# Scores from three bf16 parts on 96 rows, the causal zeros from GpSimd, and one maximum for a pair of heads

## What is computed

```python
q = (layernorm(x) @ w_q.T)  -> 16 heads of 16      # x: (16, 256, 256)
k, v = ctx @ w_k.T, ctx @ w_v.T
scores = einsum('bhqd,bhkd->bhqk', q, k) / sqrt(16)
weights = softmax(where(tril, scores, -inf))
x = x + (weights @ v) @ w_o.T
...
x = x + softmax(q2 @ k2.T / 16) @ v2               # q2, k2, v2: routed two-layer networks of layernorm(x)
```

## Time and profile before

| | us |
|---|---|
| median of three runs | 658.51 |
| lowest and highest | 652.58, 661.08 |
| span of the profiled execution, first to last instruction | 656.6 |
| own time of the profiled execution | not told apart from the three runs; the span is 1.9 below their median |
| ramp, up to the first scores of step 0 | 0 to 38.6 |
| steps 0 to 14 of the pipeline | 39.5 to 377.7 |
| step 15, the tail and the tables | 377.7 to 435 |
| routed networks | 435 to about 540 |
| second attention | about 540 to 656.6 |

### The profile page before, as it was taken

One profiled execution on the slowest core, in us unless ns is written; L12 is line 12 of the kernel. 1 busy time (PEld: TensorE's weight loads), 2 busy tenths in 40 slices (PEclk: granted clock), 3 DMA queues, 4 the chain that ended last, 5 costly groups with the idle time before them and its releaser, 6 DMA issues.

```text
span 656.6 us, 14722 instructions
## 1 busy us (share of the span) xinstructions
PE 587.3 (89%) x5119; PEld 500.4 (76%) x5119; DVE 450.4 (69%) x1511; ACT 294.5 (45%) x482; POOL 236.8 (36%) x298
## 2 busy tenths in 40 slices
PE   7588999999999999999998988849998888789996
PEld 6467787887888787788887866738887777579995
DVE  2765676998899899989888765664645544046664
ACT  3104444454545454454444452018876667333331
POOL 5700010133324233432423144413006665565642
PEclk8858999999999999999999897869999999899999
DMA  6798797889989989989977479759999998666763
GB/s 190 230 295 249 230 256 207 272 274 259 274 283 308 230 271 291 276 250 280 306 218 239 146 221 291 213 196 323 355 368 380 365 380 321 211 184 184 197 183 128
DMA packets 99639, 169.58 MB, mean 258 GB/s; under 512 B 12848, under 2 KB 67824, under 8 KB 99568
## 3 DMA queue, kind: packets, MB, share of 16 engines
q1 hardware_dynamic: 87712, 141.83, 69.2%
q0 software_dynamic: 9216, 25.18, 12.7%
q10 hardware_dynamic: 2640, 1.65, 0.9%
HBM read 92.59 MB, written 75.50 MB: 256 GB/s over the span
## 4 chain that ended last, share of the span: by engine, by line
PE 48%; DVE 14%; DMA 13%; SPq 11%; issue 8%; ACT 3%; another core or an unknown queue 2%; ACTq 1%; DVEq 0%; POOL 0%; POOLq 0%
PE banks L820 4%; PE banks L831 4%; DMA parts_dram<-k_lo 4%; DVE mneg L1188 4%; PE banks L846 4%; PE banks L892 4%; SPq L335 4%; PE banks L544 3%; DMA k<-parts_dram 3%; PE banks L913 3%; PE banks L529 3%; PE banks L556 3%; DMA xb<-xs_dram 3%; PE banks L686 3%; PE banks L716 2%
## 5 line engine op out<-in xcount | busy, mean ns | idle before, releaser
L1550 POOL DMA_INDIRECT xs_dram<-xn2s,place x96 | 95.3, 993 | 186.3 <-ACT pt L946 141.2
L946 ACT ACTIVATE pt<-banks 128x768 f32<-128x768 f32 x128 | 103.7, 811 | 102.8 <-PE banks L557 83.3
L1188 DVE TENSOR_REDUCE mneg<-banks 128x2 f32<-128x512 f32 x240 | 122.0, 549 | 34.9 <-PE banks L545 29.0
L544 PE MATMUL banks<-k,q 107*128 107x256 f32 x240 | 76.5, 370 | 15.9 <-DVE mneg L1188 9.6
L556 PE MATMUL banks<-q,k 109*128 109x256 f32 x256 | 75.0, 345 | 2.3 <-ACT pt L946 0.4
L544 PEld LDWEIGHTS banks<-k,q 107*128 107x128 f32 x240 | 46.5, 194 | 27.6 <-DVE mneg L1188 12.4
L557 PE MATMUL banks<-q,k 109*128 109x128 f32 x256 | 57.7, 225 | 0.0
L572 PE MATMUL banks<-pt,vp 128*32 128x256 f32 (+1 forms) x1024 | 56.4, 339 | 0.0
L556 PEld LDWEIGHTS banks<-q,k 109*128 109x128 f32 x256 | 49.1, 192 | 7.7 <-ACT pt L946 6.7
L545 PE MATMUL banks<-k,q 107*128 107x128 f32 x240 | 54.4, 227 | 0.0
L1537 POOL TENSOR_SCALAR ve<-mv 128x2 f32<-128x2 f32 x32 | 7.3, 228 | 127.5 <-DVE mv L1114 81.5
(11 more groups left out here) (177 smaller groups left out, 1301.7 us busy)
## 6 DMA issues: line engine op xcount, KB each, us to landing
ys_dram<-yb SPq DMA_DIRECT2D x36, 512.0 KB
xb<-xs_dram SPq DMA_DIRECT2D x35, 512.0 KB
k<-parts_dram SPq DMA_DIRECT2D x128, 128.0 KB, 4.5
q<-parts_dram SPq DMA_DIRECT2D x64, 256.0 KB, 4.3
xs_dram<-zero SPq DMA_DIRECT2D x45, 256.0 KB
xs_dram<-zero SPq DMA_DIRECT2D x18, 384.0 KB, 4.5
...
```

The source lines that it names most:

```text
L544: mm(ps[:, 0:S], q[0:KN, t, P:S], k[0:KN, t, :], start=True, stop=True)
L946: nc.scalar.activation(pt[:, 2 * p:2 * p + 2, :], st_banks(b, p)[:, :, 0:S + P], ACT.Exp, scale=SC).then_inc(exp_sb, 1)
L1188: last = nc.vector.tensor_reduce(mneg[1 - u][:, t, 2 * j:2 * j + 2], S_BANKS[:, :, cols], axis=AX.X, op=ALU.max, negate=True)
L1550: gp.indirect_dma_start(xs_dram[tree], bass.IndirectOffsetOnAxis(ap=place[:, k:k + 1], axis=0), xn2s[m % RING][:, t, :], None).then_inc(sc ...
```

## The change

- q and k are split into three bf16 parts. ACT makes the first (for q also times 2^-82) and in the pipeline the second, DVE the remainder (`remainder`), and POOL the third (`third_part`). Six products of parts stand on 96 rows, all scores are bf16 products, and `q4`, `k4` and `ct` have three buffers. A batch is projected, split and unloaded one step earlier (`LEAD` = 3 instead of 2), and each half of the heads is stacked by six transfers; a step starts by issuing the stack of `b+2`. `parts_dram` is bf16.
- `natural` makes the scores of a head in three products of 128 columns, of which the first, without a mask, uses 96 rows.
- One `tensor_reduce` for a pair of heads gives three maxima a head, and once a batch `last_maxima` joins two of them.
- The transposed scores have no mask. After each exponential POOL writes zeros above the diagonal (`causal`, an `affine_select` on 128 partitions by 4 by 128 of `pt`), and `weigh` waits for that (`pt_sb`). `pt` is 512 wide a head instead of 384.
- In the ramp three batches are projected and split, and POOL writes constants of two more buffers.

```diff
-PARTS = 4
-KS = PARTS * DK
+PARTS = 3
+PAIRED = 6
+KS = PAIRED * DK
+LEAD = 3
...
-            def unload(b, n, s, m):
...
+            def unload(b, m):
+
+                part, split = ((qp, q3_sb), (kp, k3_sb))[m]
+                if b >= BUFS:
+                    for c in range(C):
+                        sp.wait_ge(stacked[c][b % BUFS], landed(b - BUFS, c))
+                sp.wait_ge(split, b + 1)
+                sp.dma_start(parts_dram[b % BUFS][m].rearrange("r c p k -> p (r c) k"),
+                             part[b % 2][:].rearrange("p r (c k) -> p (r c) k", c=C)).then_inc(unloaded[b % BUFS], 16)
...
+                        for x, first in enumerate((0, 3 * DK, 5 * DK)):
+                            w = PARTS - x
+                            rows = src[:, 0:w] if m == 0 else src[:, x:x + 1].to_broadcast([DK, w, GROUP * S])
+                            sp.dma_start(full[z][first:first + w * DK, hs, :].rearrange("p h k -> p (h k)"),
+                                         rows).then_inc(stacked[c][z], 16)
...
+            def natural(ps, b, t):
+
+                q, k = q4[b % BUFS], k4[b % BUFS]
+                mm(ps[:, 0:P], q[0:KS, t, P:S], k[0:KS, t, 0:P], start=True, stop=True)
+                mm(ps[:, P:S], q[0:KT, t, P:S], k[0:KT, t, P:S], start=True, stop=True)
+                return mm(ps[:, S:S + P], q[0:KT, t, 0:P], k[0:KT, t, 0:P], start=True, stop=True)
...
-                pe.wait_ge(exp_sb, PAIRS * b + 2 * r + 2)
+                pe.wait_ge(pt_sb, PAIRS * b + 2 * r + 2)
...
+            def block_maxima(b, j, two):
+
+                nc.vector.tensor_reduce(mneg[b % 2][:, 2 * j:2 * j + 2, :],
+                                        two[:, :, 0:S + P].rearrange("p e (i k) -> p e i k", k=P),
+                                        axis=AX.X, op=ALU.max, negate=True).then_inc(max_sb, 1)
+
+            def last_maxima(b):
+
+                v.wait_ge(max_sb, PAIRS * (b + 1))
+                ge(v, mT_ps, b - 1)
+                nc.vector.tensor_tensor(mlast[b % 2][:], mneg[b % 2][:, :, 0], mneg[b % 2][:, :, 1], ALU.min
+                                        ).then_inc(mlast_sb, 1)
...
-                        for t, cols in ((1, slice(0, S)), (0, slice(S, S + P))):
-                            last = nc.vector.tensor_reduce(mneg[1 - u][:, t, 2 * j:2 * j + 2], S_BANKS[:, :, cols],
-                                                           axis=AX.X, op=ALU.max, negate=True)
-                        last.then_inc(max_sb, 1)
+                        block_maxima(b + 1, j, S_BANKS)
+                        if j == PAIRS - 1:
+                            last_maxima(b + 1)
...
+            def third_part(b, part, slot, second, rem, ready, done):
+
+                gp.wait_ge(ready, b + 1)
+                pool.tensor_tensor(part[b % 2][:, slot, :], rem[:], part[b % 2][:, second, :], ALU.subtract).then_inc(done, 1)
+
+            def causal(b, p):
+
+                gp.wait_ge(exp_sb, PAIRS * b + p + 1)
+                diag = pt[:, 2 * p:2 * p + 2, :].rearrange("p e (i k) -> p (e i) k", k=S)[:, :, 0:P]
+                pool.affine_select(out=diag, in_=diag, compare_op=ALU.is_ge, fill=0.0, base=0,
+                                   pattern=[[0, 2 * T], [1, P]], channel_multiplier=-1).then_inc(pt_sb, 1)
...
                 for j in range(PAIRS):
+                    if j == 0 and has(b, -1) and b < NB:
+                        causal(b - 1, 4)
+                    if j == 5 and has(b, LEAD):
+                        third_part(b + LEAD, kp, K3, K2, k_rem, k2_sb, k3_sb)
+                    if has(b, 0) and j >= lag(b):
+                        causal(b, j - lag(b))
+                    if j < LAG and has(b, -1):
+                        causal(b - 1, j + PAIRS - LAG)
                     if j in SLOTS and has(b, -4) and b < NB - 1:
                         gp.wait_ge(exp_sb, PAIRS * (b - 1) + j + (LAG + 2 if j < LAG else LAG + 1))
                         scatter(b - 4, SLOTS.index(j) // T, (SLOTS.index(j) % T,))
```

More of the change, by code:

```diff
@@ L40 @@
 EPS = 1e-5
[L41 to L45 removed]
+WIDE = 5
+QS = 2.0 ** -82
+Q_FACTOR = [2.0 ** (62 - 46 * i) for i in range(WIDE)]
+K_FACTOR = [-2.0 ** (46 * i - 121) for i in range(WIDE)]
+KM = KS + 2
+KT = KM + (P + WIDE - 1) // WIDE
+BUFS = 3
+GROUP = NH // C
 SC = DK ** -0.5
@@ L86, in build @@
         xs_dram = [nc.dram_tensor(f"xs_dram{t}", [ROWS, D], FP, kind="Internal").ap() for t in range(TREES)]
-        parts_dram = [nc.dram_tensor(f"parts_dram{i}", [2, C, 2, P, S], FP, kind="Internal").ap() for i in range(2)]
+        parts_dram = [nc.dram_tensor(f"parts_dram{i}", [2, PARTS, C, P, S], BF, kind="Internal").ap() for i in range(BUFS)]
         ys_dram = [nc.dram_tensor(f"ys_dram{t}", [ROWS, D], FP, kind="Internal").ap() for t in range(TREES)]
@@ L742, in first_scores @@
                 for e in range(2):
-                    t, ps = 2 * j + e, two[:, e, :]
-                    mm(ps[:, 0:S], q4[0][0:KN, t, P:S], k4[0][0:KN, t, :], start=True, stop=True)
-                    last = mm(ps[:, S:S + P], q4[0][0:KN, t, 0:P], k4[0][0:KN, t, 0:P], start=True, stop=True)
+                    last = natural(two[:, e, :], 0, 2 * j + e)
                 last.then_inc(s_ps, 1)
@@ L1369, in ramp @@
                     if j == 1:
[L1370 removed]
+                        norm_out(3, 1)
+                last_maxima(0)
             ramp()
@@ new lines, in factors_k @@
+                pool.memset(kw[:], K_FACTOR[WIDE - 1]).then_inc(k_factor, 1)
+                for i in range(WIDE - 1, -1, -1):
+                    gp.wait_ge(k_factor, WIDE - i)
+                    pool.affine_select(out=halves(kw[:]), in_=halves(kw[:]), compare_op=ALU.is_ge,
+                                       fill=K_FACTOR[i - 1] if i else 0.0, base=WIDE * KM - 1 - i,
+                                       pattern=[[0, T], [1, P]], channel_multiplier=-WIDE).then_inc(k_factor, 1)
+                gp.wait_ge(k_factor, WIDE + 1)
```

472 lines of the change are left out of this document (231 added, 241 removed).

## The result

The changed kernel takes 676.16 us (median of four runs, 674.18 to 677.99) where the kernel before takes 657.35: a ratio of 1.028, 95% interval 1.024 to 1.033. It is slower, and the time lies outside the range that was given.

What follows compares the result with a forecast made beforehand. PE bounds the early steps and step 13, DVE with PE's answer steps 3 to 12. Ramp +3, steps 0-2 -4.5, 3-12 +2, 12-13 -3, 14 -0.5, tail +1: -2 against 658.5, so 656.5 us; range 640 to 675.

Steps and rivals of the forecast that it cites:

- The ramp: Before step 0: 14 more DVE operations ahead of the first maxima and four POOL casts instead of two; +3 us.
- What zeros do to DVE: Steps 3 to 12: POOL's selects hold DVE's copies and `tensor_scalar` operations; 1.15 us a step, bounds 0 and 2.2.
- The rival with two-input operations: Steps 3 to 12: selects also hold DVE operations reading two SBUF inputs; 2.2 us a step, total 667 us; chance 0.22.
- The walk: Laying the eight selects where exponentials end in the earlier trace's step, to see which DVE operations they hit; 1.15 a step.
- Without anything in the way ... 0.95 shorter: Steps 3 to 12: quicker maxima and PE answers, less `last_maxima`, shorten each step 0.95 us if nothing holds DVE; 9.5 in ten.
- Scores on PE: Steps 0 to 2: bf16 products save 2.2 us of PE a step, 6.7 at most, 0 at least; taken as -4.5.
- Maxima: DVE in each step: one reduction over 768 takes 0.957 us, saving 0.065 a pair, 0.5 a step; `last_maxima` costs 0.2.
- Steps 12 to 14: End of pipeline: 12 and 13 lose projections and transposes, -3 us; step 14 has fewer waits for DVE, -0.5.
- Tail: After the pipeline: eight scatters stand ahead of the last zeros; +1 us.
- The clock: Steps 3 to 12: PE's idle pieces lower its granted clock, 1.5 us a step, +15, total 671.5; chance 0.12.
- the late case: Third parts or `weigh` behind `pt_sb` cost 2.6 us a step, about 680; chance 0.04, shared with a late stack.

Runs made afterwards that it cites:

- the memset run: Changed kernel with a POOL memset of the same 4 x 128 columns in place of each select; 656.00 us against 636.01 for the kernel before, ratio 1.031.

## Why the prediction was wrong

The forecast of 656.5 was 19.7 us too low, and the measured time is 1.2 above the range's upper end, 675. Its terms, one by one:

- **The ramp, "I take +3, bounds 0 and +8": +17.3. This is the step that failed.** The prediction read from the earlier trace rows that a cast of POOL and a `tensor_scalar` of DVE exclude each other, and used it for the selects in the steps only. In the ramp it counted the four casts of 3.6 us as POOL's own time, and of the inverse deviation of batch 3 said only that it stands behind them. It stands between the two pairs, and that of batch 2 ahead of the first. DVE's `xn` and the pair of casts are released by the same inverse deviation, so `xn` starts 0.48 and 0.36 us behind a cast and is held through both. With the casts on ScalarE step 0 starts at 42.64, 3.1 later than before: the hold, with the low clock behind it, made the other 14.2. That the 3.1 meets the +3 is in part luck: DVE's own cast of constants, put down as long as before, takes 2.29 us instead of the 5.08 that it took beside POOL's cast, so the rest of the ramp grew by more than 3.
- **What zeros do to DVE, "1.15, the kind that the trace shows".** The rival with two-input operations, given 0.22, is what happens. `place` at 204.13 and `dstep` at 277.28 are held; with a memset, which doesn't read, they are not. DVE's operations are longer by about 2.1 a step, where that rival had 2.2. By its 2.2 the ten steps would be +12.5 us, by the forecast +2; measured +9.3 (with step 12's own saving of 0.6, which the forecast counts elsewhere). The walk had also laid only the eight selects beside DVE; the third part of k beside `xn` was missed, and `xn` alone lost 0.9 a step.
- **The Trainium skill was on that side.** "SBUF - State Buffer", section "Who interferes with whom", has the rule that the memset run shows: 0.20 us for `dstep` beside an operation that only writes, 0.66 for the same operation beside a select. I had set it back because no row of before showed it.
- **"Without anything in the way ... 0.95 shorter": an understatement.** Free of selects and with the mask on PE, the ten steps take 215.1, 12.3 less than before, 1.23 a step, with 16 products more. PE's busy time was forecast as 19.5 us a step and is 20.6 in the changed kernel.
- **Scores on PE, -4.5 in steps 0 to 2: -8.6.** Starts are 58 ns apart on average (0.64 us for eleven gaps) against 55. Steps 1 and 2 gave 1.7 and 2.8, where full use of the saving would be 2.2 each; step 0 gave 4.0 and so passed the bound, with a granted clock of 0.91 instead of 0.79. The prediction took step 0 to be like the others. What the clock, the products and the removed waits for stacked parts gave of the 4.0 was not separated.
- **Maxima.** 947 ns measured for 957, `last_maxima` 0.18 for 0.2. In time it gives 0.034 a pair, half of what was put in, by the run with two reductions.
- **Steps 12 to 14, -3.5:** measured -0.6, -1.0 and -1.2, together -2.9. **Tail, +1:** +2.0; the late `weigh` of step 15, with 6.19 us of idle time ahead of it, is in it. **POOL:** a select 0.64 for 0.65, the third part 1.15 for 1.0, POOL at 14.7 a step for 14.6.
- **The clock and the late `weigh`.** The granted clock is 0.99 in the ten steps, though PE waited there for maxima up to 1.7 us at a time; that rival, with 0.12, did not happen in the steps, and in the ramp a low clock cost about 1.5 us at the projections of q. `weigh` waited for zeros once between 60 and 360 us, for 0.5 us. That the clock's 671.5 and the 680 of the late case lie nearest to the measured time says nothing for them.
